# Order and PSUM banks of the second attention's outputs in a four-stage block on one core

## What is computed

```
x = x + tanh(g_xattn[0]) * attention(layernorm(x), ctx)
x = x + tanh(g_ffn[0])   * experts(layernorm(x))          # 2 of 8 by sequence
x = x + tanh(g_xattn[1]) * autocorrelation(layernorm(x), ctx)
x = x + tanh(g_ffn[1])   * mlp(layernorm(x))              # blockwise FP4 of inputs and weights
```

## Time and profile before

| what | value |
|---|---|
| median of 3 runs | 293.07 us (292.92 to 293.31) |
| the profiled execution | 291.37 us, of which the span from first to last instruction is 289.2 us |
| mean granted TensorE clock in it | 0.976 |
| busy share of the span | PE 89%, DVE 69%, ACT 56%, POOL 41% |

### The profile page before, as it was taken

How to read it: one execution, slowest core, us unless ns; L and a number is a source line. 1 busy time by engine, 2 the same in 40 slices (tenths; PEclk the granted TensorE clock), 3 DMA queues, 4 the chain that set the end, 5 groups by cost and what they waited for, 6 DMA issues and landing times.

```text
span 289.2 us, 6270 instructions
## 1 busy us (share of the span) xinstructions
PE 257.1 (89%) x2176; PEld 200.9 (69%) x2176; DVE 199.6 (69%) x538; ACT 162.0 (56%) x370; POOL 119.2 (41%) x170
## 2 busy tenths in 40 slices
PE   7999999999899999999999998898856779767955
PEld 5655466666578779999999985556734547544855
DVE  3997678889987762522222249768758799998981
ACT  2479976666686666766666666636351724343421
POOL 4564599996202132199822105303533031313120
PEclk9999999999999999999999999999997969997999
DMA  7998000000000278776777500000000000000001
GB/s 194 376 356 345 4 3 0 2 2 2 0 3 2 82 316 341 291 297 279 303 295 295 221 0 3 0 1 2 0 0 0 2 1 0 18 18 20 19 19 57
DMA packets 12159, 30.15 MB, mean 104 GB/s; under 512 B 992, under 2 KB 5216, under 8 KB 12000
## 3 DMA queue, kind: packets, MB, share of 16 engines
q1 hardware_dynamic: 12128, 29.75, 27.3%
HBM read 9.75 MB, written 1.05 MB: 37 GB/s over the span
## 4 chain that ended last, share of the span: by engine, by line
PE 64%; DVE 16%; ACT 8%; issue 6%; DMA 3%; POOL 2%; SPq 1%; DVEq 0%; POOLq 0%
PE ps L1316 11%; PE ps L1305 11%; PE ps L1161 6%; PE ps L1494 4%; PE ps L1135 4%; DVE s_region L281 4%; PE ps L1148 4%; PE ps L1063 3%; PE ps L1436 2%; PE ps L1054 2%; PE ps L1171 2%; PE ps L1055 2%; PE ps L1353 2%; DVE s_region L1000 2%; DVE s_small L1010 2%
## 5 line engine op out<-in xcount | busy, mean ns | idle before, releaser
L575 ACT ACTIVATE s_region<-ps,s_region 128x128 f32<-128x128 f32 x144 | 41.1, 369 | 22.0 <-PE ps L1305 21.7
L871 DVE SCALAR_TENSOR_TENSOR s_ctxT<-ps,s_region,s_ctxT 128x64 f32 x72 | 18.1, 282 | 44.2 <-PE ps L1316 44.2
L1305 PE MATMUL ps<-s_region 128*128 128x128 f32 x288 | 38.5, 276 | 0.3
L1316 PE MATMUL ps<-s_region 128*128 128x128 f32 x288 | 38.0, 275 | 0.0
L288 POOL TENSOR_TENSOR s_region<-s_region,s_small 128x704 f32<-128x704 f32 (+2 forms) x13 | 17.4, 1341 | 47.3 <-DVE s_region L281 47.3
L1305 PEld LDWEIGHTS ps<-s_region 128*128 128x128 f32 x288 | 35.0, 192 | 1.0 <-DMA s_region<-s_wall 0.6
L1316 PEld LDWEIGHTS ps<-s_region 128*128 128x128 f32 x288 | 35.0, 192 | 0.2 <-issue 0.2
L253 POOL TENSOR_TENSOR s_small<-s_small,s_par 128x4 f32<-128x4 f32 (+3 forms) x14 | 15.5, 1106 | 45.2 <-DVE s_small L236 45.2
L400 POOL COPY s_region<-s_xt 128x64 f32 x72 | 14.8, 236 | 32.1 <-PE ps L1305 22.1
L1494 PE MATMUL ps<-s_region 128*128 128x352 f32 x64 | 25.0, 542 | 2.4 <-ACT s_region L652 2.3
L518 ACT COPY s_region<-ps 128x512 f32<-128x512 f32 x32 | 17.2, 593 | 16.2 <-PE ps L1148 16.2
(11 more groups left out here) (216 smaller groups left out, 507.6 us busy)
## 6 DMA issues: line engine op xcount, KB each, us to landing
s_region<-s_wall SPq DMA_DIRECT2D x36, 514.0 KB, 3.1
s_wall<-wall SPq DMA_DIRECT2D x8, 514.0 KB, 8.7
s_par<-par SPq DMA_DIRECT2D x1, 1316.0 KB, 10.9
s_x<-x SPq DMA_DIRECT2D x2, 512.0 KB, 7.2
out<-s_x SPq DMA_DIRECT2D x8, 128.0 KB, 1.8
s_region<-ffn SPq DMA_DIRECT2D x1, 560.0 KB, 3.6
s_ctxT<-ctxT SPq DMA_DIRECT2D x2, 256.0 KB, 4.6
s_ctxT<-ctxT SPq DMA_DIRECT2D x1, 512.0 KB, 7.1
```

The source lines that it names most:

```text
L575: ins = act.activation(hg[j % 3][:, c, :], ps[:, j % 3, RPT * S * c:RPT * S * (c + 1)], ACT.Gelu, bias=wbuf[j % 6][:, FF + FC * D + c:FF + ...
L871: dve.scalar_tensor_tensor(row, ps[:, 4 + j % 2, S * k:S * k + S], w, row, ALU.mult, ALU.add).then_inc(m["acc_done"], 1)
L1305: ins = mm(ps[:, j % 3, RPT * S * c:RPT * S * (c + 1)], w[:, P * c:P * c + P], xg[j % 4], start=True, stop=True)
L1316: ins = mm(ps[:, 4 + j % 2, 0:RPT * S], w[:, FF + D * c:FF + D * c + D], hg[j % 3][:, c, :], start=(c == 0), stop=(c == FC - 1))
```

## The change

It reorders instructions and spreads the outputs over banks; no instruction is added or left out.
- Head sums: PE turns half 0 ahead of summing half 1, and correlates it ahead of turning half 1; ACT copies in that order.
- Outputs 0 and 2 use bank 5, output 1 bank 1, output 3 bank 6. Output 1 waits for roll 5 (`of_done` 12), which frees bank 1, and output 2 for `attention_out(0)`; the others for no bank.
- PE: product 0 follows spectrum 4, output 0 follows spectrum 5, product 1 follows spectrum 6; the turned weights come after spectrum 7, product 2 and product 3.
- DVE: output and statistics of group 0 come ahead of rolls 6 and 7; those of group 2 ahead of x_round(0).
- POOL: powers of group 0 ahead of its last two sums, powers of group 2 ahead of x_unscale(0).
- ACT: the copies of the turned weights go one ahead of normalising group 0, one after product 2's copy, one after the first absolute value; product 3's copy goes ahead of normalising group 1, and group 2 is normalised ahead of the first copy of the turned x.
- `gate_up(0)` waits for `x3_done` 2 (bank 1 read) in place of all rolls.

```
@@ -47,6 +47,7 @@
 CTX_BANK = (4, 6, 7, 4)
 KV_BANK = (6, 7, 6, 7, 6, 7, 2, 3)
 SPEC_BANK = (0, 1, 6, 7)
+OUT_BANK = (5, 1, 5, 6)
 TOP4 = 4
 
 
@@ -432,12 +433,14 @@
                 pool.wait_ge(m["xd_done"], g + 1)
                 fp4_unscale(pool, qd[g % 2], xsc[g % 2], 4 * D // BLK, qv[g % 2]).then_inc(m["xq_done"], 1)
 
-            for q in range(PAIRS):
+            for q in range(6):
                 values_added(q)
             powers(pool, 0, 4)
+            values_added(6)
+            values_added(7)
             powers(pool, 4, 8)
+            powers(pool, 8, 12)
             x_unscale(0)
-            powers(pool, 8, 12)
             powers(pool, 12, 16)
             x_unscale(1)
             for q in range(1, PAIRS + 1):
@@ -625,12 +628,12 @@
             kv_turned(5)
             x_turned(1)
             normalise(act, 8, 12, m["xn_c"], 9)
+            normalise(act, 14, 16, m["xn_c"], 10)
             x_turned(2)
-            normalise(act, 14, 16, m["xn_c"], 10)
             x_turned(3)
             sums_read(0)
+            sums_turned(0)
             sums_read(1)
-            sums_turned(0)
             sums_turned(1)
             exp_lead(0)
             kv_turned(6)
@@ -639,10 +642,7 @@
             kv_turned(7)
             turn_gx(1)
             preload(ACT.Silu)
-            weights_turned(0)
             y1_turned(0)
-            weights_turned(1)
-            weights_turned(2)
             y1_turned(1)
 
             def turned_x(g):
@@ -668,13 +668,16 @@
                     act.wait_ge(m["xd_done"], g - 1)
                 act.activation(qm[g % 2], qv[g % 2], ACT.Abs, scale=FINE).then_inc(m["xm_done"], 1)
 
+            weights_turned(0)
             normalise(act, 0, 4, m["xn_d"], 11)
             y1_turned(2)
+            weights_turned(1)
+            y1_turned(3)
             normalise(act, 4, 8, m["xn_d"], 12)
             x_magnitude(0)
-            y1_turned(3)
+            weights_turned(2)
+            normalise(act, 8, 12, m["xn_d"], 13)
             turned_x(0)
-            normalise(act, 8, 12, m["xn_d"], 13)
             silu(0)
             x_magnitude(1)
             normalise(act, 12, 16, m["xn_d"], 14)
@@ -971,7 +974,7 @@
             def attention_out(g):
                 dve.wait_ge(m["bo_added"], g + 1)
                 dve.wait_ge(m["o_done"], g + 1)
-                dve.scalar_tensor_tensor(group(x, g), ps[:, 5, :], tg[:, 2:3], group(x, g), ALU.mult, ALU.add).then_inc(m["x3_done"], 1)
+                dve.scalar_tensor_tensor(group(x, g), ps[:, OUT_BANK[g], :], tg[:, 2:3], group(x, g), ALU.mult, ALU.add).then_inc(m["x3_done"], 1)
 
             def x_stats(g):
                 dve.wait_ge(m["x3_done"], g + 1)
@@ -1026,10 +1029,12 @@
                 x_stats(g)
 
             out_and_stats(0)
+            roll_values(6)
+            roll_values(7)
             out_and_stats(1)
             x_scale(0)
+            out_and_stats(2)
             x_round(0)
-            out_and_stats(2)
             out_and_stats(3)
             x_scale(1)
             for q in range(PAIRS + 3):
@@ -1407,10 +1412,10 @@
             queries(2)
             queries(3)
             sum_heads(0)
+            turn_sums(0)
             sum_heads(1)
-            turn_sums(0)
+            correlate(0)
             turn_sums(1)
-            correlate(0)
             correlate(1)
             context_kv(6)
             context_kv(7)
@@ -1446,8 +1451,11 @@
 
             def out_tokens(g):
                 pe.wait_ge(m["y1_ready"], g + 1)
-                pe.wait_ge(*((m["x3_done"], g) if g else (m["gx_ready"], 2)))
-                mm(ps[:, 5, :], pc("idft_o"), y1[g % 2].rearrange("p a b -> p (a b)"), start=True, stop=True).then_inc(m["o_done"], 1)
+                if g == 0:
+                    pe.wait_ge(m["gx_ready"], 2)
+                elif g < 3:
+                    pe.wait_ge(*((m["of_done"], 12) if g == 1 else (m["x3_done"], 1)))
+                mm(ps[:, OUT_BANK[g], :], pc("idft_o"), y1[g % 2].rearrange("p a b -> p (a b)"), start=True, stop=True).then_inc(m["o_done"], 1)
 
             turn_lags(0)
             spectrum(0)
@@ -1455,20 +1463,20 @@
             turn_lags(1)
             spectrum(2)
             spectrum(3)
+            spectrum(4)
+            out_product(0)
+            spectrum(5)
+            out_tokens(0)
+            spectrum(6)
+            out_product(1)
+            spectrum(7)
             turn_weights(0)
-            spectrum(4)
-            spectrum(5)
-            out_product(0)
-            spectrum(6)
-            spectrum(7)
-            turn_weights(1)
-            out_tokens(0)
-            out_product(1)
-            turn_weights(2)
             out_tokens(1)
             out_product(2)
+            turn_weights(1)
             out_tokens(2)
             out_product(3)
+            turn_weights(2)
             out_tokens(3)
             keep_clock(4, 7)
 
@@ -1484,7 +1492,7 @@
             def gate_up(q):
 
                 pe.wait_ge(m["xqt_used"], q // 2 + 1)
-                pe.wait_ge(*((m["sg_done"], q) if q else (m["of_done"], 2 * PAIRS)))
+                pe.wait_ge(*((m["sg_done"], q) if q else (m["x3_done"], 2)))
                 pe.wait_ge(m["wq_used"], 3)
                 for n in range(2):
                     if n:
```

More of the change, by code:

```diff
@@ L1457, in _ @@
             spectrum(3)
-            turn_weights(0)
-            spectrum(4)
-            spectrum(5)
-            out_product(0)
-            spectrum(6)
-            spectrum(7)
-            turn_weights(1)
-            out_tokens(0)
-            out_product(1)
-            turn_weights(2)
+            spectrum(4)
+            out_product(0)
+            spectrum(5)
+            out_tokens(0)
+            spectrum(6)
+            out_product(1)
+            spectrum(7)
+            turn_weights(0)
             out_tokens(1)
             out_product(2)
+            turn_weights(1)
             out_tokens(2)
             out_product(3)
+            turn_weights(2)
             out_tokens(3)
```

20 lines of the change are left out of this document (10 added, 10 removed).

## The result

| | before | after |
|---|---|---|
| median of 4 runs each, on the same chip (us) | 293.0 (292.9 to 293.3) | 288.77 (288.56 to 289.35) |
| profiled execution, its span (us) | 291.37, 289.2 | 288.94, 286.9 |
| mean granted clock in it | 0.976 | 0.970 |

The ratio of the runs is 0.9857 (interval 0.984 to 0.9874): 4.2 us faster by the runs, but 2.43 by the two profiled executions (291.37 less 288.94), where 2.1 was forecast. Two things have to be found, then: which steps made the 2.4, and where the other 1.8 came from.

What follows compares the result with a forecast made beforehand. The prediction took a chain of waits among PE, DVE, ACT and POOL, none full, as the bound up to the MLP's first product. Its terms, +0.74 − 4.14 + 1.3 = −2.1, gave 291.0 us from median 293.07; range 288.7 to 292.9.

Steps and rivals of the forecast that it cites:

- Outputs and rolls: Second attention's outputs up to the MLP: first output at 205.15 instead of 207.52, MLP's first product 4.14 earlier.
- Head sums: Second attention's head sums, a loss: PE turns the first lags 0.74 later, as the context's products start 0.96 late.
- The clock: First gate and up: low clock after PE's idle costs 1.3, so the MLP's first product is only 2.1 earlier.
- the rival without a low clock: No low clock on gate and up: 289.7, 288.4 if a later wait goes too; chance 0.18 shared with head sums gaining.
- What that product gains, the end gains: MLP's first product on DVE: from 226.61 DVE is nearly always at work, so any gain there reaches the end.
- The port: DVE's rounding of x beside POOL's power: no hold, 0; rival that it waits: 0.85, total 291.8, chance 0.12.
- The sum: Whole kernel: +0.74 − 4.14 + 1.3 = −2.1, taken from the median 293.07: 291.0, or 289.3 for a profiled execution.
- The 1.70: Whole kernel before: how far the runs' median, 293.07, lies above the profiled execution, 291.37; left unexplained.
- rivals which the profiled execution doesn't show: Faster side of the range, down to 288.7: the faster rivals with most of DVE's later wait at 267.38 gone.

Runs made afterwards that it cites:

- all rolls first: Kernel after with DVE rolling all eight pairs, and POOL adding them, ahead of the first output and powers again: 294.58, one run.
- one bank: Kernel after with all four outputs in bank 5 again, each waiting until DVE has read the one before: 289.88 over 10 runs, ratio 0.993.
- the part alone: Kernel before with only the head sums in the new order on PE and ACT: 292.92 over 12 runs, ratio 1.003.
- third trace of after: Another traced execution of the kernel after, nothing changed: 288.97, 111.8 from the first expert output to the last output.
- lower group: Runs of the unchanged kernel before at 290.5 to 291.9, its profiled execution among them; lower-group means 291.1 before, 288.5 after.
- the upper: Runs of the unchanged kernel before at 292.6 to 293.9; means of such slower runs 293.3 before, 290.7 after.
- execution 4: One more traced execution of the kernel before, nothing changed: 293.03.
- execution 2: One more traced execution of the kernel before, nothing changed: 291.23.
- the normalising alone: Kernel before with only the normalising of tiles 14 and 15 put ahead of ACT's `x_turned(2)`: 291.22 over 12 runs, ratio 0.9971.

## Why the prediction was right and wrong

- **Outputs and rolls**: right. Lags to first output 9.0 (forecast 8.9), first output to the turn of x 13.3 (13.25). The mechanism was the place of the first output (all rolls first undoes it); the banks, which the forecast credited with freeing the fourth output, bring nothing of their own (one bank).
- **Head sums**: right in sign and cause, mis-sized: 0.9 for 0.74. A turn alone held PE for 1.04 up to its next start (190.26 to 191.30 in the part alone), where the forecast took 0.92, half of what two turns in a row take. The turns and the two waits for ACT, 0.70 and 0.46 in the part alone, made the context's products 1.1 late, counted from the first expert output, instead of 0.96. They did hold the lags: with the last of them moved behind, the lags came 1.1 earlier.
- **An edit that was not costed**: the normalising ahead of `x_turned(2)`. It was part of the diff, and PE's wait of 0.62 for L244 stood in the trace of before; the rows of PE that the prediction draws on begin at 189.97. A term put at nothing, without a reason: it is worth 1.0, and it made up for the head sums.
- **The clock**: right that the low level would move from the fourth output and the fillers onto gate and up, and mis-sized: 1.7 for 1.3 in the profiled execution. In the third trace of after it is not there at all: the same wait (2.63), then gate and up in 5.13. Two of three executions paid it, so the rival without a low clock was not a rival to the forecast but a share of its runs.
- **"What that product gains, the end gains"**: it held in the profiled execution (0.2 was lost behind the product), not as a rule. In the third trace the product came 4.1 earlier than before and the last output 2.1, as low stretches further on took the rest. That the forecast's 1.3 for the clock fits the end is in part luck: with or without the low clock on the first gate and up, after ended within 0.5.
- **The port**: right to take 0, for the power (below).
- **The sum**, the step that failed. "I take the difference from the median" set a difference found in an execution of the lower group against a median of runs of the upper. The 1.70 of which "no row says why" was kept for the kernel after; it was the distance between the groups, and by their times the first four runs of after all fell in the lower one, where their median (288.77) lies 0.17 under the profiled execution (288.94). 291.37 less 2.1 is 289.3, which the prediction itself gave for a profiled execution, and the four runs after had a median of 288.77. That 288.77 still lies in the range, at its very edge of 288.7, is luck: that edge was meant for rivals which the profiled execution doesn't show. In equal conditions the change made 2.3 where 2.1 was forecast, but by terms that cancel: the normalising's 1.0 left out on one side, and on the other 0.4 too little for the clock and 0.1 to 0.2 each for the head sums, for the way from the lags to the first output and for the MLP behind its first product.

## What to carry to other kernels

Count times from the last mark that the change can't touch before comparing two executions: here the stretch ahead of it varies by 2.9 us between executions (172.3 to 175.2), more than the change is worth. Walk the diff line by line, one term for each hunk, a moved pointwise instruction too: PE's short wait for it is seen only if its timeline is read from there on. When an early consumer is put between the parts of a loop, look at what its producer's engine does with the time: here PE's idle time moved ahead of the costliest matmuls, and keeping PE at work in it, with one product of the context moved, together brought about as much again as the change (285.96 beside 288.9).

## What the runs showed of the hardware

- One program ran PE at half speed at different places in different executions. Its first products took 2.05 or 1.10. In the first attention the granted clock fell to 0.50 with PE busy in the whole of the 3 us shown, after an idle of 1.06 at 75.87 (execution 4), and not after 0.93 at 75.58 (execution 2). Behind equal idle times of 3.65 it fell in all six traces of before and not with the normalising alone, and behind 2.63 it fell in two traces of after and not in the third. No run tells what decides.
- POOL's power started 0.25 ahead of DVE's rounding, ran beside it, and neither was longer than elsewhere (1.01, 1.42). The short product behind it took 0.64, for 0.21 in the chain of before, and ended at 217.21, with the rounding's second instruction (217.16). POOL after, then the same instruction in the chain of waits of before:

```profile
215.49 1.01 POOL L254 TENSOR_TENSOR s_small<-s_small,s_par 128x4 f32<-128x4 f32 x1 [2.88 <-DVE s_small L237]
216.57 0.64 POOL L256 TENSOR_TENSOR s_small<-s_small 128x4 f32<-128x4 f32 x1
217.24 1.06 POOL L289 TENSOR_TENSOR s_region<-s_region,s_small 128x512 f32<-128x512 f32 x1
```
```profile
214.44 0.21 POOL s_small L255
```

POOL waited for the rounding anyway (L289 starts at 217.24), so it cost nothing. The Trainium skill, "SBUF — State Buffer", section "SBUF: two separate sides", gives the port that DVE and POOL share to whichever starts first, for its whole instruction: by it the rounding would have waited for the power, and the short product for the rounding's second instruction. The trace agrees for the short product (0.64 instead of 0.21), and not for the rounding, which started 0.25 after the power and ran beside it.
